# Decoder kernel on one core: row tiles in the second attention's weighting, weight preparation moved out of the stages' beginnings, semaphores cleared by the next stage, lead-in in another order

## The chip, the core and the metric

The kernel runs on one core of a Trainium2 chip. The metric is the device time of one execution in microseconds, the median of three runs. All weights and activations come in as fp32 in DRAM, and the output is fp32.

## The reference

Sixteen sequences of 112 tokens with 1024 features go through two decoder layers, each with a self part, a cross attention with 32 heads over 375 context rows, and a feed-forward part, each with a layernorm behind it:

```
x = _layernorm(x + _L0_attn_ref(x, mask, weight, bias))       # one linear, 32x32 blocks of the weight masked out
x = _layernorm(x + _L0_xattn_ref(x, ctx, ctx, 0, mask_ff0))   # 32 heads of 32, 8 key/value heads, 375 context rows
x = _layernorm(x + _L0_ffn_ref(x, Wq, Wr, aux_keys, aux_values, Wvd, Wvu, Wu1, ...))   # top 8 of 256 slots, gated
x = _layernorm(x + _L1_attn_ref(x, weight_qkv, weight_proj))  # 32 heads of 128, 8 key/value heads, causal over 16
x = _layernorm(x + _L1_xattn_ref(x, ctx, ctx, 0, mask_ff0))
x = _layernorm(x + _L1_ffn_ref(x, A_w, B_w, Wq_w, keys))      # 64 experts of rank 8, top 16
```

In `_L0_attn_ref` a 32x32 block of the weight counts if the sum of the int32 mask over it is above zero. In `_L1_attn_ref` the attention runs over the axis of 16 sequences, so that for each of the 112 positions there is a causal 16x16 table of probabilities per head, and

```
attn = softmax(where(causal, q k^T / sqrt(128), min))
out  = (attn v).reshape(S, B, 32*128) @ weight_proj.T
```

## The kernel before

Linears are computed in fp32 by three products of parts: each operand is split into a high part, rounded to the fp32r format, and a low part, the rest; high times high, high times low and low times high are summed in PSUM. Each such product is one pass of TensorE (a `MATMUL` row each). A few small products are plain fp32, which show two `MATMUL` rows each.

`build` runs three stages, one behind the other, each with its own semaphores and on-chip buffers: `token_stage` for layer 0 (from the start to about 847 us), `self_attention` for layer 1 (to about 2689 us), and `token_stage` for layer 1 (to the end). Behind each stage the helper `stage` runs a block in which GpSimd clears the stage's semaphores one by one (L1682 to L1686), and the next stage's engines start behind it.

**token_stage.** It starts with a preparation (L176 to L321) in a block of its own, which every engine leaves at L321 before the main part begins. SP loads chunks of 128 rows in the order of `part_of` into six stage buffers, which are the buffers `attn`, `row`, `xnew`, `xcur`, `probs` and `masked` of the main part (L238). In layer 0 the chunks are eight of the int32 mask, sixteen of Wu1 and Wq, and eight of the linear's weight. DVE sums the mask chunks (L311), ACT makes high parts (L250), DVE the low ones (L319), and for the linear's weight DVE multiplies by the block mask first (L314). In between PE and DVE compute the small tables of the slot router (L257 to L294), whose inputs ACT's queue loads (`small`). In layer 1 the chunks are the expert matrices A (eight) and B (four), and PE computes the router's keys (L269).

The main part is software-pipelined over turns t = -2 to B+1 = 17. Each of 16 sequences goes through its steps in several turns, and in a turn each engine runs 32 steps n, one per head of sequence t: scores (PE L545), mask and row minimum (DVE L835), exp (ACT L747), transposes of the probabilities (PE L550, copied at ACT L742 or DVE L829) and their product with V (PE L564). The other work of the neighbours, the first linear of sequence t+2 (PE L536), its layernorm (L510, L518), the queries (L527), keys, the feed-forward part (L646 to L674 on PE, L890 to L925 on DVE) stands between the heads at fixed n. SP's queue carries all loads and stores of a turn in a hand-written order: in turn t it loads x and its transpose for t+2, keys and queries from DRAM in layouts repeated for the heads (L370, L387), stores new queries and context parts (L380, L410), and loads `xcur` (L424), the row that is added to the heads' output. The scores of turn t start when queries (t, half 0) have landed; DVE has the row `L_masked L835 <- DMA L_xcur` where a turn's DVE work waits for `xcur`.

**self_attention.** The 1792 rows are taken as two halves of seven chunks of 128 rows; a chunk holds 8 positions of 16 sequences. A group G is one key/value head of a half, 16 in all. A group has units K, V and four Q, each a product of the half's rows with a 1024x128 weight (L1309, 24 passes of 512 columns and 24 of 384, `product` called from `unit`). Then `scores` (L1330) with 32-column tiles for the block-diagonal scores, `softmax` on DVE (L1564 to L1582, with ACT's exp L1451) and a stream transpose that gives `probsT`, whose entries outside the 32x32 blocks on the diagonal are zero. The next part runs in `project`, during the next group, right after its K unit:

```
1345  pe.matmul(bank("pv", G, c), val[:, c, :], probsT[:, :, c, :], start=True, stop=True).then_inc(pv_ok, 1)
```

one for each chunk c, into a ring of three PSUM banks that the projection uses too. ACT takes the high part (L1465), DVE the low (L1587, `low_weighted`), into three buffers `o_hi` and `o_lo`, and PE multiplies by the projection weights (L1358, 24 passes of 512 columns for each chunk), DVE adds to the rows (L1599). The PE order is weigh(0), weigh(1), project(0), weigh(2), project(1) and so on. GpSimd splits all weights of the stage from two raw buffers which SP loads (L1254, L1256, one split 3.4 us), in the order of the list `splits`.

Before group 0 stands a lead-in: gate and row data are loaded (L1189 to L1200), for each of seven chunks ACT doubles the row (`twice`, L1422), DVE adds the gated slot values that PE made from 64-row tiles (L1283, L1538) and takes the statistics, GpSimd the root, ACT normalizes (L1426), PE transposes (L1297), and ACT and DVE split (L1439, L1557).

## Time and profile before

| | us |
|---|---|
| median of 3 runs | 3425.71 |
| the runs | 3422.53, 3425.71, 3430.13 |
| the profiled execution, its own time | 3425.54 |
| its span | 3423.8 |
| PE busy | 3172.0 (93%) |
| weight loads busy | 2604.7 (76%) |
| DVE busy | 1849.2 (54%) |
| ACT busy | 1322.2 (39%) |
| POOL busy | 833.0 (24%) |

Columns of a timeline row are start, duration, engine, line, operation, output and input, shape and count, and in brackets the idle time before it with what ended it. Matmuls are pipelined, so the distance of two starts says what one costs, and the duration includes its tail. An engine with a q behind its name is its sequencer, which issues DMAs and waits on semaphores. GB/s is what the DMA engines moved, and DMA share how busy the 16 of them were. PEclk of 1.00 is 2.4 GHz and 0.50 is 1.2 GHz.

### The profile page before, as it was taken

The numbers are of one execution on the slowest core, as the hardware profiler recorded it, in microseconds if no ns is written. First come the engines' busy times: TensorE is split into PE (matmuls) and PEld (weight loads), VectorE is DVE, ScalarE is ACT, GpSimd is POOL, SyncE is SP. The second block draws the span as 40 slices with busy tenths as digits, with TensorE's granted clock in tenths as the row PEclk, the third lists the DMA queues.
The fourth block names the chain that finished last, engine by engine and source line by source line (L and its number), as shares of the span: only waits on it lengthen the run. The fifth ranks groups of instructions, "written<-read, shape, count | busy, mean of one in ns | idle before, by whom it ended". The sixth has DMA issues, their size and how long they took to land. (4 is left out here: it accounts for less than half of the span.)

```text
span 3423.8 us, 65971 instructions
## 1 busy us (share of the span) xinstructions
PE 3172.0 (93%) x25336; PEld 2604.7 (76%) x25336; DVE 1849.2 (54%) x4739; ACT 1322.2 (39%) x3550; POOL 833.0 (24%) x729
## 2 busy tenths in 40 slices
PE   3899999996799999999999999999999499999997
PEld 2777877775488887888878888888887378888886
DVE  4688888885443324333343323332333388888886
ACT  2577777774311111111111111111111287777774
POOL 0122222211234322432234322432232001000100
PEclk9999999997699999999999999999999799999999
DMA  5877777761322112221143111211111476655551
GB/s 181 218 177 184 172 178 181 179 171 40 94 86 87 52 53 68 87 74 44 56 154 130 45 36 50 62 52 42 38 56 31 141 175 153 152 149 144 145 138 45
DMA packets 209449, 370.01 MB, mean 108 GB/s; under 512 B 27009, under 2 KB 160737, under 8 KB 209138
## 3 DMA queue, kind: packets, MB, share of 16 engines
q1 hardware_dynamic: 205392, 363.01, 39.0%
q8 instruction: 203, 3.33, 0.4%
q10 hardware_dynamic: 3746, 2.79, 0.3%
q14 instruction: 108, 0.88, 0.1%
HBM read 283.20 MB, written 82.52 MB: 107 GB/s over the span
## 5 line engine op out<-in xcount | busy, mean ns | idle before, releaser
L747 ACT ACTIVATE L_probs<-L_masked,L_least 112x375 f32<-112x375 f32 x1024 | 624.8, 612 | 105.4 <-DVE L_least L835 102.1
L835 DVE CUSTOM_DVE_ANT_0 L_masked<-L_scores,L_nmask 112x375 f32<-112x375 f32 x1024 | 550.8, 543 | 158.2 <-PE L_scores L545 120.5
L1309 PE MATMUL sa_feat<-sa_x_hi,sa_w_hi 128*128 128x512 f32 (+1 forms) x1536 | 567.1, 369 | 1.8 <-DVE sa_x_lo L1557 1.8
L1309 PE MATMUL sa_feat<-sa_x_hi,sa_w_lo 128*128 128x512 f32 (+1 forms) x1536 | 561.4, 365 | 0.0
L1309 PE MATMUL sa_feat<-sa_x_lo,sa_w_hi 128*128 128x512 f32 (+1 forms) x1536 | 560.1, 365 | 0.0
L550 PEld LDWEIGHTS L_turned<-L_ident,L_probs 112*125 112x125 f32 x3072 | 456.3, 190 | 129.7 <-issue 46.5
L550 PE MATMUL L_turned<-L_ident,L_probs 112*125 112x112 f32 x3072 | 533.2, 283 | 19.5 <-DVE L_probsT L829 16.0
L545 PE MATMUL L_scores<-L_krep,L_qrep 128*112 128x376 f32 x1024 | 418.5, 410 | 6.8 <-DMA L_qrep<-query_parts 6.3
L1358 PE MATMUL sa_ring<-sa_p_hi,sa_o_hi 128*128 128x512 f32 x896 | 387.8, 433 | 8.3 <-issue 8.3
L742 ACT COPY L_probsT<-L_turned 125x336 f32<-125x336 f32 x672 | 293.2, 436 | 228.2 <-PE L_turned L550 227.5
L1599 DVE TENSOR_TENSOR sa_acc<-sa_acc,sa_ring 128x512 f32<-128x512 f32 x224 | 154.2, 688 | 414.8 <-PE sa_ring L1358 414.8
L1358 PE MATMUL sa_ring<-sa_p_lo,sa_o_hi 128*128 128x512 f32 x896 | 354.2, 395 | 0.0
L1358 PE MATMUL sa_ring<-sa_p_hi,sa_o_lo 128*128 128x512 f32 x896 | 354.1, 395 | 0.0
L1564 DVE SCALAR_TENSOR_TENSOR sa_sm<-sa_score,sa_causal 128x224 f32<-128x224 f32 x64 | 25.0, 391 | 549.8 <-PE sa_score L1330 549.8
L1309 PEld LDWEIGHTS sa_feat<-sa_x_hi,sa_w_hi 128*128 128x128 f32 x1536 | 289.7, 189 | 40.3 <-issue 6.8
L1309 PEld LDWEIGHTS sa_feat<-sa_x_hi,sa_w_lo 128*128 128x128 f32 x1536 | 289.3, 188 | 31.5
L1309 PEld LDWEIGHTS sa_feat<-sa_x_lo,sa_w_hi 128*128 128x128 f32 x1536 | 289.6, 189 | 30.3
L1465 ACT CAST sa_o_hi<-sa_ring 128x512 fp32r<-128x512 f32 x112 | 65.7, 586 | 496.8 <-PE sa_ring L1345 496.8
L467 POOL TENSOR_TENSOR L_attn<-L_attn,L_xcur 112x512 f32<-112x512 f32 x64 | 82.3, 1286 | 630.0 <-DVEq L848 630.0
L1256 POOL TENSOR_TENSOR sa_w_lo<-sa_raw,sa_w_hi 128x1024 fp32r<-128x1024 f32 x96 | 230.1, 2397 | 14.5 <-issue 1.0
L1358 PEld LDWEIGHTS sa_ring<-sa_p_hi,sa_o_hi 128*128 128x128 f32 x896 | 168.5, 188 | 78.0 <-issue 41.3
L1254 POOL CAST sa_p_hi<-sa_raw 128x1024 fp32r<-128x1024 f32 x64 | 68.6, 1073 | 604.9 <-PE sa_ring L1358 594.9
(305 smaller groups left out, 5240.9 us busy)
## 6 DMA issues: line engine op xcount, KB each, us to landing
L_qrep<-query_parts SPq DMA_DIRECT2D x256, 224.0 KB, 6.2
sa_raw<-in_wqkvU_dram SPq DMA_DIRECT2D x96, 512.0 KB, 3.6
L_krep<-ctx_parts SPq DMA_DIRECT2D x256, 188.0 KB, 4.3
sa_raw<-in_wprojU_dram SPq DMA_DIRECT2D x64, 512.0 KB, 3.6
query_parts<-L_qT_hi SPq DMA_DIRECT2D x64, 224.0 KB, 6.5
query_parts<-L_qT_lo SPq DMA_DIRECT2D x64, 224.0 KB, 6.8
L_xcur<-x SPq DMA_DIRECT2D x32, 448.0 KB, 5.0
L_val<-in_ctx_dram SPq DMA_DIRECT2D x64, 187.5 KB
```

The lines of the kernel that those rows point to most:

```text
L467: p.tensor_tensor(attn[0:S, cols], attn[0:S, cols], xcur[0:S, cols], ALU.add).then_inc(sum_ok, 1)
L545: pe.matmul(scores[0:S, (NH * t + n) % 3, 0:TP], qrep[:, gq, r, gi, :], krep[:, 4 * gq + gi, :], start=True, stop=True).then_inc(score_ok, 1)
L550: mm = pe.transpose(turned[0:TC, m % 2, S * j:S * j + S], probs[0:S, m % 4, TC * j:TC * j + TC], ident[0:S, 0:S])
L742: nc.scalar.copy(probsT[:, m % 8, :, :], turned[0:TC, m % 2, 0:TJ * S].rearrange("p (j s) -> p j s", s=S)).then_inc(copied_s, 1)
L747: nc.scalar.activation(probs[0:S, e % 4, :], masked[0:S, e % 4, :], ACT.Exp, bias=least[0:S, e:e + 1], scale=-1.0, accum_out=rsum[0:S, e:e ...
L835: v.tensor_tensor_reduce(out=masked[0:S, n % 4, :], in0=scores[0:S, (NH * t + n) % 3, 0:T], in1=nmask[0:S, :], scale=1.0, scalar=HUGE, op0 ...
L1254: nc.gpsimd.tensor_copy(hi, src)
L1256: nc.gpsimd.tensor_tensor(lo, src, hi.bitcast(F32), ALU.subtract).then_inc(p_ok if u is None else unit_ok, 1)
L1309: mm = pe.matmul(feat[:, u % 2, i, 0:t.stop - t.start], a[:, u % 2, k, :], b[:, k, t], start=(n == 0), stop=(n == 3 * KT - 1))
L1358: mm = pe.matmul(out, a[:, j, c % 3, :], b[:, j, 512 * h:512 * h + 512], start=(i == 0), stop=(i == 3 * QPG - 1))
L1465: nc.scalar.copy(o_hi[:, :, c % 3, :], ring[:, slot["pv", G, c][0], :].rearrange("p (j t) -> p j t", j=QPG)).then_inc(o_hi_ok, 1)
L1599: v.tensor_tensor(acc[:, c, cols], acc[:, c, cols], ring[:, b, :], ALU.add).then_inc(ring_free[b], 1)
```

## The change

**Row tiles.** `weigh` computes each chunk by four matmuls, one for each 32 rows of the chunk, which write 128 columns each to four PSUM banks. The zeros outside the diagonal blocks are left out. The PSUM tensors are one, `banks`; the four target banks are those of `feat` and `score`, so the ring holds the projection alone; `o_hi` and `o_lo` have two buffers. The first `weigh` of a group stands inside the second product of the next group's K unit, the others each one projection ahead, behind a wait for the low part of the chunk before. ACT signals `key_ok` after the first half of K.

```diff
@@ weigh
-                pe.matmul(bank("pv", G, c), val[:, c, :], probsT[:, :, c, :], start=True, stop=True).then_inc(pv_ok, 1)
+                    if not ends_half(G):
+                        pe.wait_ge(key_ok, G + 2)
+                else:
+                    pe.wait_ge(o_lo_ok, NC * G + c)
+                for p in range(4):
+                    q = slice(32 * p, 32 * p + 32)
+                    mm = pe.matmul(banks[:, 1 + p, 0:P], val[q, c, :], probsT[q, :, c, q], start=True, stop=True)
+                mm.then_inc(pv_ok, 1)
@@ project
-                weigh(G, 0)
-                weigh(G, 1)
+                if ends_half(G):
+                    weigh(G, 0)
                 pe.wait_ge(p_ok, QPG * (G + 1))
                 for c in range(NC):
-                    pe.wait_ge(o_lo_ok, NC * G + c + 1)
+                    if c + 1 < NC:
+                        weigh(G, c + 1)
+                    else:
+                        pe.wait_ge(o_lo_ok, NC * G + c + 1)
@@ K unit of the next group
-                        unit(G, K_UNIT, lambda: scores(G - 1, QPG - 1))
+                        unit(G, K_UNIT, lambda: scores(G - 1, QPG - 1), {6: lambda: weigh(G - 1, 0)})
```

On PE, at the end of the K unit of group 1 (`sa_feat` and `sa_banks` are the PSUM tensors of the attention before and after, `sa_probsT` the transposed probabilities), the order before is

```order
L1309 MATMUL sa_feat<-sa_x_hi,sa_w_lo 128x384
L1345 MATMUL sa_ring<-sa_probsT,sa_val 128x512 x2
L1358 MATMUL sa_ring<-sa_p_hi,sa_o_hi 128x512
L1358 MATMUL sa_ring<-sa_p_lo,sa_o_hi 128x512
L1358 MATMUL sa_ring<-sa_p_hi,sa_o_lo 128x512
```

and after it is

```order
L1409 MATMUL sa_banks<-sa_x_hi,sa_w_lo 128x384
L1451 MATMUL sa_banks<-sa_probsT,sa_val 128x128 x4
L1409 MATMUL sa_banks<-sa_x_hi,sa_w_hi 128x384
L1409 MATMUL sa_banks<-sa_x_lo,sa_w_hi 128x384
L1409 MATMUL sa_banks<-sa_x_hi,sa_w_lo 128x384
L1409 MATMUL sa_banks<-sa_x_hi,sa_w_hi 128x384
L1409 MATMUL sa_banks<-sa_x_lo,sa_w_hi 128x384
L1409 MATMUL sa_banks<-sa_x_hi,sa_w_lo 128x384
L1451 MATMUL sa_banks<-sa_probsT,sa_val 128x128 x4
L1468 MATMUL sa_banks<-sa_p_hi,sa_o_hi 128x512
```

The group's first weighting has moved ahead of the last six passes of K, and the second now waits for the low part of the first.

**Preparation, layer 0.** The block is gone. At turn -2 SP loads the transposed x, eight mask chunks and eight weight chunks; DVE runs `masked_weights`, ACT `high_weights`, and PE `first_linear`, which follows the chunks k by k for both halves of the output. The tables and Wu1, Wq are loaded in turn 0, split there by GpSimd, and PE and ACT compute the small tables at fixed heads of turn 0 (`slot_tables`).

```diff
+            def load_tables():
+                sp.wait_ge(chunk_done, 2 * KT)
+                for k in range(2):
+                    sp.dma_start(wu_raw[k], io["wu1T"][512 * k:512 * k + 512].rearrange("(k p) n -> p k n", p=P)).then_inc(ld_u, 16)
+                sp.dma_start(wq_raw, io["wqT"].rearrange("(k p) n -> p k n", p=P)).then_inc(ld_u, 16)
+                for dst, src in tables:
+                    sp.dma_start(dst, src).then_inc(ld_tables, 16)
...
+            def slot_tables(n):
+                if n == 14:
+                    pe.wait_ge(ld_tables, 16 * len(tables))
+                    pe.matmul(spare[0:48, 0:SLOTS], wrT[:], keysT[:], start=True, stop=True).then_inc(rk_ok, 1)
+                if n == 18:
+                    pe.wait_ge(rkT_ok, 1)
+                if n in (18, 20):
+                    j = n // 20
+                    for k in range(KT):
+                        mm = pe.matmul(spare[:, BOT * j:BOT * j + BOT], valT[k][:, P * j:P * j + P], wvdT[:, k, :],
+                                       start=(k == 0), stop=(k == KT - 1))
...
+            def first_linear(w):
+                pe.wait_ge(split_x, w.next(split_x))
+                for k in range(KT):
+                    pe.wait_ge(chunk_done, KT + k + 1)
+                    for h, bank in enumerate((spare, wide[:, 1, :])):
+                        mm = products(bank[0:S, :], (x_hi, x_lo), (w0_hi, w0_lo), slice(512 * h, 512 * h + 512), KT,
+                                      3 * k, 3 * k + 3)
```

On SP, in turn 0 of layer 0, the queries of sequence 1's second half are stored and `xcur` is loaded behind the second load of keys and queries. Before:

```order
L387 DMA L_qrep<-query_parts 32x4x448 x4
L380 DMA query_parts<-L_qT_hi 128x448
L380 DMA query_parts<-L_qT_lo 128x448
L380 DMA query_parts<-L_qT_hi 128x448
L380 DMA query_parts<-L_qT_lo 128x448
L410 DMA ctx_parts<-L_c_hi 128x376 x2
L410 DMA ctx_parts<-L_c_lo 128x376 x2
L412 DMA L_craw<-in_ctxT_dram 128x750
L374 DMA L_val<-in_ctx_dram 125x3x128
L424 DMA L_xcur<-x 112x1024
```

After:

```order
L271 DMA L_qrep<-query_parts 32x4x448 x4
L289 DMA L_attn<-in_wu1T_dram 128x4x256
L289 DMA L_row<-in_wu1T_dram 128x4x256
L290 DMA L_oT<-in_wqT_dram 128x8x64
L292 DMA L_wrT<-in_wrT_dram 64x48
L292 DMA L_keysT<-in_keysT_dram 64x256
...
L292 DMA L_ra<-in_valuesT_dram 128x256 x2
L264 DMA query_parts<-L_qT_hi 128x448
L264 DMA query_parts<-L_qT_lo 128x448
...
L332 DMA L_xcur<-x 112x1024
```

Nineteen loads, 2.95 MB, now stand ahead of those stores and of `xcur`.

**Preparation, layer 1.** GpSimd splits the expert matrices in groups 8 to 15 of the attention (eight more splits), SP stores both parts to DRAM (8 MB), and ACT's queue loads the parts of A at the start of turn 0 and those of B at the start of turn 1 of the last stage. The router's keys are computed at turn -1.

```diff
+        if G >= NKV:
+            splits.append((G, EXPERT, G - NKV))
...
+            def load_expert(i):
+                chunks = slice(4 * i, 4 * i + 4)
+                for dst, src in (((a_hi, "expert_hi"), (a_lo, "expert_lo")), ((b_hi, "expert_hi"), (b_lo, "expert_lo")))[i]:
+                    act.dma_start(dst[:].rearrange("p k n -> p (k n)").bitcast(F32),
+                                  io[src][:, chunks, :].rearrange("p m n -> p (m n)")).then_inc((ld_a, ld_b)[i], 16)
```

**Semaphores.** No block stands between the stages. GpSimd clears those of layer 0's stage in the attention's group 2, those of the attention at the start of the last stage, and those of the last stage at the end.

```diff
-            fn(*args, sem)
-            with nc.Block() as block:
-                @block.gpsimd
-                def _(pool):
-                    for one in used:
-                        pool.sem_clear(one)
...
+    held0, sems0 = stage(token_stage, nc, 0, io, [])
+    held1, sems1 = stage(self_attention, nc, io, sems0)
+    held0.close()
+    held2, sems2 = stage(token_stage, nc, 1, io, sems1)
```

**Lead-in of the attention.** `twice` and the later doubling at half 1 are gone (the gate is halved and the epsilon of these layernorms is a quarter, which gives the same normalized rows). The gate's data are loaded first, the first weights earlier, and GpSimd splits the first two units before it takes the roots.

## Rows read from the trace of the kernel before

**Rows 1.** The page: span, and busy time of the first engine.
```profile
span 3423.8 us, 65971 instructions
...
PE 3172.0 (93%) x25336; PEld 2604.7 (76%) x25336; DVE 1849.2 (54%) x4739; ACT 1322.2 (39%) x3550; POOL 833.0 (24%) x729
```

**Rows 2.** Timeline of DVE, from the start to the first layernorm.
```profile
14.84 1.22 DVE L311 TENSOR_REDUCE L_once_brow<-L_row 128x32 f32<-128x1024 int32 x1 [0.25 <-DMA L_row<-in_bmaskT_dram]
...
34.37 1.23 DVE L314 TENSOR_TENSOR L_attn<-L_attn,L_once_bm 128x1024 f32<-128x1024 f32 x1
...
51.60 1.23 DVE L319 TENSOR_TENSOR L_w_lo<-L_row,L_w_hi 128x1024 fp32r<-128x1024 f32 x1
...
76.08 2.55 DVE L518 TENSOR_SCALAR L_xnew<-L_xb,L_mv,L_rstd 112x1024 f32<-112x1024 f32 x1 [1.06 <-POOL L_rstd L462]
```

**Rows 3.** Timeline of PE, the same stretch.
```profile
22.96 1.22 PE L257 MATMUL L_wide<-L_once_brow,L_once_blocks 128*128 128x256 f32 x2 [22.96 <-DMA L_nmask<-in_mask_dram]
...
59.86 0.77 PE L536 MATMUL L_spare<-L_w_hi,L_x_hi 128*112 128x512 f32 x1 [26.02 <-POOL L_x_lo L503]
```

**Rows 4.** Table by stretches: window, length, busy times, PEclk, DMA share, GB/s.
```profile
0.00:26.00 26.00, 3.04 (x8) 1.61 (x9) 13.21 (x23) 4.56 (x13) 0.19 (x4) 1.00 0.91 301
...
100.00:130.00 30.00, 29.41 (x232) 24.13 (x233) 16.52 (x51) 18.87 (x55) 2.52 (x2) 0.86 0.97 235
130.00:145.00 15.00, 10.62 (x102) 8.40 (x100) 13.62 (x36) 10.90 (x33) 4.10 (x4) 0.92 0.40 99
```

**Rows 5.** Waits of DVE in 100 to 145 us: total, times, longest.
```profile
DVE L_masked L835 <- DMA L_xcur<-x: 3.4, 1, 3.4
```

**Rows 6.** Waits of SP's queue, the whole span.
```profile
SPq L1682 <- PEq L1682: 17.1, 3, 6.4
```

**Rows 7.** Timeline of PE in the attention's lead-in.
```profile
861.92 0.59 PE L1366 MATMUL sa_feat<-sa_lsum,sa_ones 128*128 128x1 f32 x2 [15.78 <-ACT sa_lv L1475]
...
865.38 3.78 PE L1283 MATMUL sa_ring<-sa_wvu,sa_zT 64*128 64x512 f32 x6
...
876.55 3.78 PE L1283 MATMUL sa_ring<-sa_wvu,sa_zT 64*128 64x512 f32 x4
```

**Rows 8.** Timeline of PE in group 3, scores and weighting.
```profile
1306.17 1.09 PE L1297 MATMUL sa_ring<-sa_ident,sa_late 128*128 128x128 f32 x8
1307.02 0.48 PE L1309 MATMUL sa_feat<-sa_x_hi,sa_w_hi 128*128 128x512 f32 x1
...
1316.58 0.40 PE L1309 MATMUL sa_feat<-sa_x_hi,sa_w_lo 128*128 128x512 f32 x1
1316.91 0.70 PE L1330 MATMUL sa_score<-sa_kT,sa_qT 128*32 128x32 f32 x56
1317.54 0.50 PE L1309 MATMUL sa_feat<-sa_x_hi,sa_w_hi 128*128 128x512 f32 x1
...
1333.40 1.02 PE L1345 MATMUL sa_ring<-sa_probsT,sa_val 128*128 128x512 f32 x2
...
1334.49 0.40 PE L1358 MATMUL sa_ring<-sa_p_lo,sa_o_hi 128*128 128x512 f32 x1
...
1339.86 1.02 PE L1345 MATMUL sa_ring<-sa_probsT,sa_val 128*128 128x512 f32 x2
```

**Rows 9.** Timeline of DVE in group 2: a softmax step beside GpSimd's work.
```profile
1186.04 2.28 DVE L1570 TENSOR_TENSOR sa_sm<-sa_sm,sa_most 128x224 f32<-128x224 f32 x1
```

**Rows 10.** Timeline of PE and SP at the last stage's beginning.
```profile
2721.49 1.01 PE L527 MATMUL L_wide<-L_ident,L_xnew 112*128 112x112 f32 x4 [14.02 <-DMA L_xnew<-x]
...
2697.02 0.33 SPq L238 DMA_DIRECT2D L_attn<-in_awT_dram  x1
...
2717.63 0.34 SPq L416 DMA_DIRECT2D L_xnew<-x  x1
```

**Rows 11.** Table by stretches, turn 0 and turn 1 of the last stage.
```profile
2725.00:2765.00 40.00, 24.86 (x240) 20.37 (x240) 20.46 (x70) 23.71 (x75) 1.28 (x1) 0.73 0.93 216
2765.00:2795.00 30.00, 27.92 (x329) 23.03 (x328) 23.95 (x78) 25.62 (x80) 2.06 (x3) 1.00 0.79 186
```

More of the change, by code:

```diff
@@ L222, in token_stage @@
-        small += [(ident[:], io["ident"]), (nmask[0:S, :], io["mask"])]
-        small_in, chunk_done, prep_pe, prep_dve = s("small_in"), s("chunk_done"), s("prep_pe"), s("prep_dve")
-        chunk_in = [s(f"chunk_in{i}") for i in range(NST)]
-        chunk_masked, chunk_hi = s("chunk_masked"), s("chunk_hi")
-        prep = once.enter_context(nc.Block())
-        def chunk(i):
-            what = part_of[i][2]
-            raw = stage[i % NST][:, 0:part_of[i][1]]
-            return raw.bitcast(I32) if what == "sum" else raw
@@ L401, in body @@
                     load_queries(t, 1)
+                if first and t == 0:
+                    load_tables()
                 if on(1):
@@ L504, in body @@
                     pool.drain().then_inc(xt_free, 1)
+            for one in stale:
+                pool.sem_clear(one)
             turns(pool, body)
@@ L803, in routed_ffn, with load_small, high_weights @@
                     nc.scalar.copy(z_hi[:, :, :], spare[:, 0:4 * S].rearrange("p (j s) -> p j s", s=S)).then_inc(z_hi_ok, 1)
+            def load_small():
+                if first:
+                    act.dma_start(blocks[:], io["blocks"]).then_inc(ld_blocks, 16)
+                for dst, src in small:
+                    act.dma_start(dst, src).then_inc(small_in, 16)
+            def high_weights():
+                for k in range(KT):
+                    act.wait_ge(chunk_masked, k + 1)
+                    nc.scalar.copy(w0_hi[:, k, :], stage[(KT + k) % NST]).then_inc(chunk_hi, 1)
@@ L813, in body @@
                         routed_ffn(w, n, on)
+            load_small()
             turns(act, body)
@@ L1026, in body @@
                         routed_ffn(t, w, n, on)
+            v.memset(half[:], -0.5)
             if first:
+                for part in (c_hi, c_lo):
+                    v.memset(part[:, :, T:TP].bitcast(F32), 0.0)
+                v.memset(qaug[BOT:BOT + 1, :], 1.0)
                 dve.sem_inc(z_stored, 16)
@@ L1218, in _ @@
                 load_raw(i)
+                store_experts(i - 2)
+            for i in range(len(splits) - 2, len(splits)):
+                store_experts(i)
             store_rows(1)
+            sp.wait_ge(expert_stored, 32 * 8)
             sp.wait_ge(stored, 2 * 16 * NC)
@@ L1321, in unit @@
                 product(G, u, 0, {3: landed})
-                product(G, u, 1)
+                product(G, u, 1, later)
             def scores(G, j):
@@ L1475, in _, with take_z @@
             nc.scalar.activation(lv[:], pair[:, :, 1], ACT.Ln, bias=1.0, scale=1.0, accum_out=lsum[:]).then_inc(log_ok, 1)
-            for half in range(2):
+            def take_z(half):
                 act.wait_ge(z_ok, half + 1)
```

425 lines of the change are left out of this document (240 added, 185 removed).

## The prediction, made before the changed kernel ran

> **What bounds the kernel.** The page comes first. TensorE is busy for 3172.0 of 3423.8 us [rows 1], so the time is TensorE's own work plus about 250 us in which it waits, and a change pays where it takes passes off TensorE or shortens one of those waits. The timelines then say where the waits are: at the beginnings of the three stages. At the start the matmuls of the first linear begin at 59.86, behind 26.02 us of idle [rows 3]; between 2697 and 2721 the last stage has almost nothing but its preparation [rows 10]; the clearing blocks take 17.1 us of SP's time in three waits [rows 6]. Last I read what one chunk of the attention's weighting costs [rows 8]. The profiled execution took 3425.54 us and the median is 3425.71, so the sum made against the first holds for the second.
>
> **Layer 0's preparation.** Before, the mask sums of DVE end at 14.84 + 1.22 = 16.1, but the product with the block matrix starts at 22.96, since PE waited for all small loads [rows 2, 3], and the first masked weight chunk is made at 34.37, behind the splits of Wu1 and Wq and the small tables. Now nothing stands between: 16.1, plus 1.2 for the product, 0.4 for the comparison and some signals, and 1 us for the transposed x that is loaded first, makes about 19. The 16 DVE steps from 34.37 to 52.8 take 18.5 us [rows 2] and stay, ending at 37 to 38. The loads keep pace: some 8.9 MB (sixteen chunks of 512 KB, x and the small ones) at 301 GB/s [rows 4] are 30 us, and the last chunk is wanted at about 34. PE follows chunk by chunk with six passes each, so behind the last chunk stand six passes (0.77 us at most, [rows 3]) instead of 48, and two instead of one statistics. Before, from the last low part to the layernorm L518 there were 76.08 - 52.8 = 23.3 us; I take 5.5 (the six passes with their tail some 3, the second statistics and the root, for which L518 waited 1.06 us [rows 2], the rest). The layernorm then starts at about 43 in place of 76.08: **-33 us** (-36 to -28). What follows it, up to the first scores, is a chain through DRAM and is the same.
>
> **The tables in turn 0.** Nineteen loads with 2.95 MB are issued ahead of the query stores and of `xcur`. Just there the DMA engines are 0.97 busy at 235 GB/s [rows 4], so the loads delay the others by 2.95 / 0.235 = 12.6 us, if nothing gives. Behind them, 130 to 145 us has a share of 0.40, and that slack could take some; against it, PE now waits at head 14 for every table, with 18 heads of the turn behind it, and DVE already waited 3.4 us for `xcur` there [rows 5], which comes later now. GpSimd's six split steps on 128x1024 and 128x512 are hidden unless the turn is held by them. **+13** (+6 to +20). If the loads fitted in the slack this would be nothing, if they came as slowly as small rows can it would be 20.
>
> **Boundary 0 to 1.** The clears leave the path between the stages: one of the three waits, the longest, is 6.4 us [rows 6]. **-6.4.** In group 2 GpSimd clears them in the time that it waits for TensorE anyway.
>
> **Attention's lead-in.** Seven ACT doublings go, and loads and splits come sooner, but the chain per chunk goes through DVE, GpSimd's root, ACT, PE and back. The roots now wait for two splits of 3.4 us. **-3** (-7 to +3).
>
> **The row tiles.** From 1334.49 to the next weighting at 1339.86 stand 23 passes, 0.2335 us each; the period of a chunk is 1339.86 - 1333.40 = 6.46, and less 24 passes (5.60) the weighting costs 0.86 us [rows 8]. That is two fp32 passes of 512 columns. Now it is four matmuls of 128 columns, eight passes. A pass of 128 columns costs 0.85 / 8 = 0.106 (eight L1297 between 1306.17 and 1307.02). If the four tiles ran together it would be 2 x 0.106 = 0.21; if one after the other, 0.85. Do tiles of different rows run together here? Six L1283 in the lead-in, on both row halves, take 3.78 us, and four on one half also 3.78 [rows 7], so yes, at least two. A change of tiling has a price: the scores with 32-column tiles start 0.33 after the pass before, where 0.23 is usual, and the next pass is 0.63 behind, of which some 0.1 again is the way back [rows 8]; with two changes that is 0.2. So 0.21 + 0.2 = 0.41 at the least, and with 0.1 for what eight issues and loads in four groups add I take 0.50, near the lower end since both rows show tiles running together. The saving is 0.36 x 112 = **-40 us** (-50 with 0.41; with 0.63 as in the first rival -26).
>
> The Trainium skill, TensorE: Matmul & The Clock Gate, Part 3 (packing small matmuls), gives 3.07x for four row tiles of 512 columns, not 4x; the estimate from that page would be 0.85 / 3.07 + 0.2 = 0.48 and the same saving within 2 us. TensorEngine Tiling, Key Properties, says that changing the tiling mode drains TensorE; the trace agrees by the 0.1 us at each side of the scores, and a drain that cost more would be the last rival.
>
> The wait behind a group's first weighting, for its high and low part, stays about as long: before, the second weighting's 0.86 us stood in it, now six passes of K with 384 columns do, 6 x 0.2335 x 384 / 512 = 1.05 us. In the other chunks the low part is made during the projection before. But the first weighting also stands 1.05 us sooner behind the softmax, which is longer where GpSimd works beside it: one of its steps takes 2.28 us then [rows 9], and groups 8 to 15 get a GpSimd split more. If each of 14 groups lost all of the 1.05 it would be 15; with the splits in one group of two and hitting the last softmax seldom I take **+2** (0 to +7).
>
> **Boundary 1 to 2.** Before, SP's first load of the stage is at 2697.02 and that of `xnew`, which starts the real work, at 2717.63 [rows 10]. The preparation's 19.2 us between (less 1.4 for issues that stay) go, and the clears: the two other waits share 17.1 - 6.4 = 10.7 us [rows 6], 5.3 each. **-24.5** (-27 to -19).
>
> **Expert parts in turns 0 and 1.** Each of these turns gets 4 MB more. In turn 0 DMA is 0.93 busy at 216 GB/s, in turn 1 0.79 [rows 11]. Loads of 128 wide rows move faster than that mixture, at 301 GB/s [rows 4]: 4 MB are 13.3 us. In turn 0 I count all of them but two, since queries and keys come later by that much; in turn 1 the idle share of 0.21 over some 40 us takes 8.4 of them, and I count 3 of the rest. **+14** (+5 to +24). Final clears of fewer semaphores: **-0.4**.
>
> **Sum.** -33 + 13 - 6.4 - 3 - 40 + 2 - 24.5 + 14 - 0.4 = -78.3, that is 3425.5 - 78.3 = **3347 us**.
>
> **Rivals.**
> First, the tiles' weight loads go one after the other (eight of about half of 0.106 us) and only the streaming overlaps: 0.43 + 0.2 = 0.63 us per chunk, saving 26, not 40: 3361. For it: no row shows two weight loads at once, and the L1283 rows with long streams would look alike in both cases; against it nothing but the forecast's simplicity, so it gets a good chance.
> Second, no overlap at all: 0.85 + 0.2 = 1.05, +21 in place of -40: 3347 + 61 = 3408. The L1283 rows speak against it, but they are two tiles of 64 rows at 1.2 GHz, not four of 32.
> Third, the other side: every row tile waits until the one before has drained. A lone small pass takes 0.59 / 2 = 0.295 us [rows 7]; eight are 2.4 us for a chunk, +1.5 each, 168 us in all: 3347 + 40 + 168 = 3555. It decides for slower as soon as a chunk's weighting costs more than 0.86 + 38.3 / 112 = 1.20 us.
> Fourth, the moved loads cost nothing (the turns have slack after all): 3347 - 27 = 3320. Or they cost double, since turn 0 holds up everything behind it: 3374. The shares of 0.40 to 0.97 [rows 4, 11] leave both open.
> That the gain at the beginnings isn't there (the first scores wait for something else, as for keys) is part of the second half of that.
>
> **Chances.** Forecast with its neighbours 0.50, weight loads in series 0.20, no overlap 0.07, draining 0.04, moved loads nearly free 0.09, loads double 0.10. Terms added at their good ends give about 3312, at their bad ends with the first rival about 3390; the range is 3308 to 3390, which leaves out draining, most of no overlap, and the far ends of the loads. Some 0.2% is 7 us, about what a measurement can tell from no change; only 0.02 of the chance falls there, between the second and third rivals. Faster 0.93, same 0.02, slower 0.05.
>
> **What would show it.** The successor of the layernorm L518 at 43 us and all that follows it 33 us sooner; turn 0 of the first stage some 13 us longer; the attention's first K product 9 us sooner against the end of the stage before; a chunk period of 6.1 us in the projection, and about 0.5 from a row of four tiles to the next pass; the last stage's first transpose, at 2721.49 before [rows 10], some 24 us sooner against the attention's end. A chunk period above 6.3, or beginnings that come sooner while the turns behind them grow by as much, would make the prediction wrong.

## The result, and the profile after

| | before | changed |
|---|---|---|
| median, us | 3426.45 (4 runs) | 3375.59 (4 runs) |
| all runs, us | 3422.53, 3425.71, 3427.20, 3430.13 | 3370.88, 3371.77, 3379.40, 3379.68 |
| profiled execution, its span | 3425.54, 3423.8 | 3379.68, 3377.9 |
| ratio changed to before | | 0.9847, 95% interval 0.9834 to 0.9859 |

The changed kernel is 51 us faster. The forecast was 78 us faster, 3347, with a range of 3308 to 3390: sign and range hold, and 27 us of the expected gain are missing. The question of this section is where they went. The page of the changed kernel, as [rows 1]:

```profile
span 3377.9 us, 67066 instructions
...
PE 3153.8 (93%) x26008; PEld 2601.9 (77%) x26008; DVE 1861.0 (55%) x4698; ACT 1304.2 (39%) x3520; POOL 872.9 (26%) x751
```

TensorE has 18 us less to do (3172.0 before), so more than half of the gain is less waiting. A ladder of marks, the same places read in both timelines, gives each part's share. "First scores" is the start of DVE's first step on them, and the attention's products are the high times high passes of K, V and Q. The column "changed again" is a second profiled execution of the changed kernel (`changed_again`, 3368.71 us, below).

| stretch | before | changed | changed again | predicted change |
|---|---|---|---|---|
| start to the first scores | 101.7 | 70.1 | 70.2 | -33 |
| turn 0 of layer 0 | 42.9 | 60.4 | 58.8 | +13 |
| turns 1 to 14 | 629.3 | 629.5 | 630.9 | 0 |
| turn 15's first scores to the attention's first product | 134.8 | 125.5 | 125.5 | -9.4 |
| to its last K, V or Q product | 1721.0 | 1693.4 | 1689.5 | -38 |
| to the last stage's first scores | 110.9 | 87.7 | 86.3 | -24.5 |
| its turns 0 and 1 | 65.4 | 88.4 | 88.6 | +14 |
| turns 2 to 14 | 533.8 | 533.4 | 533.5 | 0 |
| turn 15's first scores to the end of DVE | 74.3 | 80.2 | 74.2 | 0 |

**The beginning.** Timeline of DVE of the changed kernel, as [rows 2]:

```profile
15.75 1.22 DVE L1048 TENSOR_REDUCE L_brow<-L_row 128x32 f32<-128x1024 int32 x1
...
18.85 1.23 DVE L1063 TENSOR_TENSOR L_xnew<-L_xnew,L_bm 128x1024 f32<-128x1024 f32 x1
...
36.01 2.25 DVE L1056 TENSOR_TENSOR L_w_lo<-L_xcur,L_w_hi 128x1024 fp32r<-128x1024 f32 x1
...
43.73 2.55 DVE L444 TENSOR_SCALAR L_xnew<-L_xb,L_mv,L_rstd 112x1024 f32<-112x1024 f32 x1 [1.06 <-POOL L_rstd L370]
```

The first masked chunk is made at 18.85 (19 predicted), the last low part ends at 38.3 (37 to 38), the layernorm starts at 43.73 (43). The only surprise is the last low part, 2.25 us instead of 1.22. GpSimd adds the bias beside it, but the two DVE steps before it lie beside the same work and took 1.21 us each, so the cause isn't shown.

**Turn 0 of layer 0.** Waits of PE between 69 and 131 us, with total, times and longest:

```profile
PE L_spare L543 <- DMA L_ra<-in_valuesT_dram: 11.4, 1, 11.4
PE L_wide L453 <- DVE L_xnew L444: 5.6, 1, 5.6
```

L543 is the first of the small tables at head 14, and it stands 11.4 us for the last of the nineteen loads. Table by stretches, columns as [rows 4]:

```profile
35.00:45.00 10.00, 3.74 (x14) 1.94 (x13) 8.68 (x9) 1.91 (x2) 6.51 (x5) 0.96 0.00 0
75.00:95.00 20.00, 12.67 (x114) 10.38 (x112) 9.66 (x28) 8.91 (x27) 5.39 (x4) 0.93 1.02 210
```

The DMA share is 1.02 while the tables are waited for, and 0.00 in a stretch some 30 us before they are asked for.

**The weighting.** Timeline of PE in the attention, changed kernel, as [rows 8]:

```profile
1302.75 0.40 PE L1468 MATMUL sa_banks<-sa_p_hi,sa_o_lo 128*128 128x512 f32 x1
1303.08 0.50 PE L1451 MATMUL sa_banks<-sa_probsT,sa_val 32*128 32x128 f32 x8
1303.51 0.50 PE L1468 MATMUL sa_banks<-sa_p_hi,sa_o_hi 128*128 128x512 f32 x1
1303.85 0.39 PE L1468 MATMUL sa_banks<-sa_p_lo,sa_o_hi 128*128 128x512 f32 x1
...
1309.30 0.50 PE L1451 MATMUL sa_banks<-sa_probsT,sa_val 32*128 32x128 f32 x8
```

A chunk's period is 1309.30 - 1303.08 = 6.22 us (6.46 before), and less 24 x 0.2335 the weighting costs 0.62 us, where 0.50 was predicted. The eight passes take 0.43 to the next full pass. The rest stands on the two sides: 0.33 from the pass before, where 0.23 is usual, and again 0.34 behind the first full pass.

**Turns 0 and 1 of the last stage.** DMA issues of the changed kernel between 2656 and 2667 us, with count, KB of each and the time to landing:

```profile
L_a_hi<-expert_hi ACTq DMA_DIRECT2D x1, 2048.0 KB, 15.0
L_a_lo<-expert_lo ACTq DMA_DIRECT2D x1, 2048.0 KB, 22.6
L_qrep<-query_parts SPq DMA_DIRECT2D x4, 224.0 KB, 8.4
L_krep<-ctx_parts SPq DMA_DIRECT2D x4, 188.0 KB, 20.6
```

and of the kernel before at the same place of its turn, 2727 to 2737 us:

```profile
L_krep<-ctx_parts SPq DMA_DIRECT2D x8, 188.0 KB, 7.4
L_qrep<-query_parts SPq DMA_DIRECT2D x5, 224.0 KB, 7.8
```

The keys of the second half, issued in the same microseconds as the two large loads, take 20.6 us instead of 7.4. (Before, the median is over eight key loads, with the changed kernel over four.) PE waits for the queries queued behind them (total, times and longest, 2628 to 2760 us):

```profile
PE L_scores L471 <- DMA L_qrep<-query_parts: 13.6, 2, 6.9
```

**The end.** The profiled execution is one of the two long ones. Table by stretches of the changed kernel, from some 42 us behind the last turn's first scores:

```profile
3330.00:3338.00 8.00, 7.49 (x60) 5.27 (x57) 3.95 (x8) 1.17 (x3) 1.29 (x1) 1.00 0.00 0
3338.00:3346.00 8.00, 5.70 (x27) 4.38 (x26) 5.00 (x9) 1.06 (x2) 1.56 (x4) 0.72 0.19 58
3346.00:3354.00 8.00, 8.00 (x33) 6.56 (x33) 2.41 (x13) 0.35 (x1) 0.00 (x0) 0.64 0.01 3
```

The granted clock falls from 2.4 to 1.2 GHz within the second stretch; PE was busy for 7.49 of 8 us in the first and for 5.70 in the second. The profile of the kernel before has 2.4 GHz at the same place, and its last stretch is 5.9 us shorter (74.3 us against 80.2).

### The profile page after: what moved, and what is told of

It reads as the page before. It is cut to its first block and busy times, and to the rows that moved or that the text cites. A ratio compares the mean times of both kernels' runs of the same rounds, so it can differ in the third digit from the quotient of the medians.

```text
span 3377.9 us, 67066 instructions
## 1 busy us (share of the span) xinstructions
PE 3153.8 (93%) x26008; PEld 2601.9 (77%) x26008; DVE 1861.0 (55%) x4698; ACT 1304.2 (39%) x3520; POOL 872.9 (26%) x751
## 5 line engine op out<-in xcount | busy, mean ns | idle before, releaser
L1409 PE MATMUL sa_banks<-sa_x_hi,sa_w_hi 128*128 128x512 f32 (+1 forms) x1536 | 568.6, 370 | 1.8 <-DVE sa_x_lo L1661 1.8
L1409 PE MATMUL sa_banks<-sa_x_hi,sa_w_lo 128*128 128x512 f32 (+1 forms) x1536 | 561.4, 366 | 0.0
L1409 PE MATMUL sa_banks<-sa_x_lo,sa_w_hi 128*128 128x512 f32 (+1 forms) x1536 | 560.0, 365 | 0.0
L471 PE MATMUL L_scores<-L_krep,L_qrep 128*112 128x376 f32 x1024 | 419.8, 411 | 17.1 <-DMA L_qrep<-query_parts 13.6
L1468 PE MATMUL sa_banks<-sa_p_hi,sa_o_hi 128*128 128x512 f32 x896 | 366.0, 408 | 0.0
L1468 PE MATMUL sa_banks<-sa_p_lo,sa_o_hi 128*128 128x512 f32 x896 | 356.1, 397 | 0.0
L1468 PE MATMUL sa_banks<-sa_p_hi,sa_o_lo 128*128 128x512 f32 x896 | 355.8, 397 | 0.0
L1409 PEld LDWEIGHTS sa_banks<-sa_x_hi,sa_w_hi 128*128 128x128 f32 x1536 | 289.6, 189 | 42.0 <-issue 6.8
L1409 PEld LDWEIGHTS sa_banks<-sa_x_hi,sa_w_lo 128*128 128x128 f32 x1536 | 289.3, 188 | 31.6
L1409 PEld LDWEIGHTS sa_banks<-sa_x_lo,sa_w_hi 128*128 128x128 f32 x1536 | 289.5, 188 | 30.2
L490 PE MATMUL L_wide<-L_probsT,L_val 125*32 125x112 f32 x6144 | 203.3, 266 | 8.5 <-DMA L_val<-in_ctx_dram 7.9
```

What stands on the lines that cost most here:

```text
L471: pe.matmul(scores[0:S, (NH * t + n) % 3, 0:TP], qrep[:, gq, r, gi, :], krep[:, 4 * gq + gi, :], start=True, stop=True).then_inc(score_ok, 1)
L490: mm = pe.matmul(wide[HD * gi:HD * gi + HD, gq, S * r:S * r + S], val[:, j, HD * g:HD * g + HD], probsT[:, (4 * u + gi) % 8, j, :], start= ...
L1409: mm = pe.matmul(feat[u % 2][i][:, 0:t.stop - t.start], a[:, u % 2, k, :], b[:, k, t], start=(n == 0), stop=(n == 3 * KT - 1))
L1468: mm = pe.matmul(out, a[:, j, c % 2, :], b[:, j, 512 * h:512 * h + 512], start=(i == 0), stop=(i == 3 * QPG - 1))
```

## The experiments

**Row tiles undone, places kept** (`full_rows`):

```diff
-                    mm = pe.matmul(banks[:, 1 + p, 0:P], val[q, c, :], probsT[q, :, c, q], start=True, stop=True)
+                    mm = pe.matmul(banks[:, 1 + p, 0:P], val[:, c, :], probsT[:, :, c, q], start=True, stop=True)
```

> The changed kernel with one edit: each of the four weighting matmuls of a chunk takes all 128 rows (the same 128 output columns, the zeros outside the diagonal blocks included), so no row tiles; places, banks and waits stay. In the changed kernel's profile a chunk of the projection has a period of 6.22 us, of which the weighting is 0.62. Theory A (row tiles gain only in that a load and a stream of different rows overlap, and the eight weight loads come one after the other): eight whole passes of 0.106 us each without change of tiling are 0.85 us, the chunk's period 6.45, 112 x 0.23 = 26 us more than the changed kernel. Theory B (the gain in the attention comes from the new places and the projection's own ring, not from the tiles): the period stays near 6.22 and the time within 5 us of the changed kernel.

Measured: 3415.12 us, ratio to before 0.9958 (0.9944 to 0.9972), against 3371.46 for the changed kernel on the same chip, 44 us slower. Its chunk:

```profile
1308.00 1.05 PE L1451 MATMUL sa_banks<-sa_probsT,sa_val 128*128 128x128 f32 x8
1308.81 0.48 PE L1468 MATMUL sa_banks<-sa_p_hi,sa_o_hi 128*128 128x512 f32 x1
...
1314.49 1.05 PE L1451 MATMUL sa_banks<-sa_probsT,sa_val 128*128 128x128 f32 x8
```

The period is 6.49, more than the 6.45 expected; no wait shows in it. From first to last product the attention takes 1728.7 us: 39.2 more than in `changed_again` and 35.3 more than in the first profile of the changed kernel, and 7.7 more than the kernel before. A part of each difference is the clock: this profile has 1.2 GHz for 21.7 us of the attention, `changed_again` for 13.6, the first profile for 18.9 and the kernel before for 15.6. If such a stretch costs half of its length (an estimate; `changed_again` shows it below), the tiles alone are worth about 34 to 35 us, and the new places and banks cost about 5 without them. What they cost is 0.035 us of each chunk's period and a wait of 0.45 us for the low part before each group's second weighting. Another 5 us of the whole difference are the clock at the end (79.0 us behind the last turn's first scores, not 74.2). Theory B is out. Theory A has the period nearly right and the time not (26 us), and its reason is wrong, as the next runs show.

**One row tile for all four** (`one_group`):

```diff
+                    mm = pe.matmul(banks[:, 1 + p, 0:P], val[0:32, c, :], probsT[0:32, :, c, q], start=True, stop=True)
```

> The changed kernel, but all four weighting matmuls of a chunk take rows 0 to 31 of the values and of the probabilities, so that all lie on one row tile (three quarters of the weighted values are thus not the reference's). If different row tiles are what makes them overlap: eight passes of about 0.106 us, 0.85 plus 0.2 for two changes of tiling, a chunk's period of 6.65 us, and 48 us more in all. If a tile of 32 rows is cheaper in itself, wherever it lies: the period stays 6.22.

Measured in one execution: 3445.68 us, 74 us above the changed kernel, period 6.88:

```profile
1315.11 1.15 PE L1451 MATMUL sa_banks<-sa_probsT,sa_val 32*128 32x128 f32 x8
1316.19 0.50 PE L1468 MATMUL sa_banks<-sa_p_hi,sa_o_hi 128*128 128x512 f32 x1
...
1321.99 1.15 PE L1451 MATMUL sa_banks<-sa_probsT,sa_val 32*128 32x128 f32 x8
```

A tile of 32 rows isn't cheaper in itself; different rows are the gain. It costs even 0.23 us more than expected. The single records say where: the first two passes start 0.213 us apart, the other six 0.110 to 0.112. One weight load, 0.107 us, isn't hidden behind the change of tiling; the next run shows that it is the first pass's own. On the way back another isn't hidden, that of the full matrix.

**Streams twice as wide** (`wide_stream`):

```diff
+                    w = slice(64 * (p // 2), 64 * (p // 2) + 64)
+                    mm = pe.matmul(banks[:, 1 + p, 0:2 * P], val[q, c, :], probsT[q, :, c, w], start=True, stop=True)
```

> The changed kernel, but each row tile's matmul streams 256 columns instead of 128 (twice as many tokens of the chunk; the copies take the first 128, so the weighted values are not the reference's). The weight loads are as before. Theory A (the eight weight loads of 128 columns in series set the 0.43 us between the first tile and the next full pass; streams of different tiles overlap): the chunk's period grows by under 0.1 us, mostly the tail of the last tile. Theory C (the streams themselves come one after the other and loads are hidden behind them): 8 x 0.053 = 0.43 us more per chunk, period 6.65, 48 us in all.

Measured in one execution: 3397.14 us, 26 above the changed kernel; period 6.44, 0.22 more:

```profile
1304.28 0.71 PE L1452 MATMUL sa_banks<-sa_probsT,sa_val 32*128 32x256 f32 x8
1304.92 0.50 PE L1469 MATMUL sa_banks<-sa_p_hi,sa_o_hi 128*128 128x512 f32 x1
...
1310.71 0.71 PE L1452 MATMUL sa_banks<-sa_probsT,sa_val 32*128 32x256 f32 x8
```

Neither theory: A wanted under 0.1, C 0.43. It is 0.107 for each of two passes, so two streams are on the path, not eight and not none. The records of `changed_again` fit that. One row from each of four timelines, of the weight loads and of PE, with windows that hold the first pass alone, then the second alone:

```profile
1306.72 0.20 PEld L1451 LDWEIGHTS sa_banks<-sa_probsT,sa_val 32*128 32x128 f32 x4 [0.36 <-issue]
1306.73 0.39 PE L1451 MATMUL sa_banks<-sa_probsT,sa_val 32*128 32x128 f32 x4
1306.83 0.20 PEld L1451 LDWEIGHTS sa_banks<-sa_probsT,sa_val 32*128 32x128 f32 x4
1306.94 0.29 PE L1451 MATMUL sa_banks<-sa_probsT,sa_val 32*128 32x128 f32 x4
```

Within 0.02 us all four tiles have their loads and their matmuls under way, each 7 ns behind the one before. The second loads start at 1306.833 to .853, the second matmuls at 1306.940 to .960. So the four tiles run wholly side by side, loads too. These two passes alone allow two readings of the first 0.213 us: stream, then the second load, or the first load, then the stream with the second load beside it. The wide run decides, by the same rows:

```profile
1304.28 0.20 PEld L1452 LDWEIGHTS sa_banks<-sa_probsT,sa_val 32*128 32x128 f32 x4 [0.37 <-issue]
1304.38 0.20 PEld L1452 LDWEIGHTS sa_banks<-sa_probsT,sa_val 32*128 32x128 f32 x4
1304.60 0.39 PE L1452 MATMUL sa_banks<-sa_probsT,sa_val 32*128 32x256 f32 x4
```

The second loads start 0.11 us behind the first here too, though the streams are twice as long, and the second matmuls 0.21 us behind these loads, the length of a stream of 256 columns. So the second loads run beside the first streams, and what isn't hidden is the first load, with which the first matmul's record begins. What the path sees in the changed kernel is about 0.09 us until the pass before is through, load 0.107, two streams of 0.107, about 0.09 again, and the load of the next full matrix, 0.11, which wasn't made ahead either: together the 0.62. The expectation of the next run takes the first reading.

**The tiles twice** (`two_sets`): this tells whether the load shows in every pass or only behind a change of tiling.

```diff
-                for p in range(4):
+                for p in (0, 1, 2, 3, 0, 1, 2, 3):
```

> The changed kernel, but each chunk's four row tiles are computed twice, one set right behind the other (the second overwrites the first with the same values). The chunk's period is 6.22 us now; in its trace the four tiles of a pass start 7 ns apart, their loads too, the second pass starts 0.213 us behind the first, and 0.107 of this is the second pass's weight load, which starts only when the first pass has streamed. Theory L (each pass of a row tile shows its weight load): 2 x 0.213 = 0.43 us more per chunk, period 6.65. Theory F (the load shows only once, in the first pair behind a change of tiling, since nothing could be loaded ahead; after that 0.107 to 0.112 a pass, as on the single row tile): 0.21 to 0.24 more, period 6.45.

Measured in one execution: 3403.00 us; periods of 6.455 us (rows of the same timeline):

```profile
1305.63 0.73 PE L1451 MATMUL sa_banks<-sa_probsT,sa_val 32*128 32x128 f32 x16
...
1312.09 0.73 PE L1451 MATMUL sa_banks<-sa_probsT,sa_val 32*128 32x128 f32 x16
```

Theory F, to the hundredth: +0.235. A second set of four tiles costs 0.11 per pass, since its loads run under the streams of the first. Of the 0.62 us of a chunk's weighting, two streams are 0.21; the rest is what two changes of tiling cost, among it two loads of 0.11 that aren't hidden.

**The changed kernel again** (`changed_again`):

> The changed kernel itself, beside the others on the same chip, as their measure. Its four executions so far fall in two pairs, 3371 and 3379.5 us; the profiled one was of the longer kind and shows a granted clock of 1.2 GHz between 3341 and 3352 us, where the kernel before still had 2.4 GHz. If the pairs come from that alone, these executions again lie at one or the other, and a profile of the shorter kind shows no such fall and about 74 us from the last turn's first scores to the end, not 80.

Measured: 3368.71, 3370.00, 3372.92 and 3380.27 us, median 3371.46, ratio 0.9838 (0.9823 to 0.9853). The profiled execution took 3368.71:

```profile
3325.00:3333.00 8.00, 7.49 (x60) 5.27 (x57) 3.98 (x8) 1.13 (x3) 1.29 (x1) 1.00 0.00 0
3333.00:3341.00 8.00, 5.70 (x42) 4.57 (x41) 5.01 (x10) 1.07 (x2) 1.56 (x4) 1.00 0.19 58
3341.00:3349.00 8.00, 5.94 (x27) 4.13 (x27) 3.69 (x15) 0.88 (x2) 0.00 (x0) 1.00 0.01 2
```

The same stretch, the same busy time of 7.49 and 5.70 us, and the clock stays at 2.4 GHz; 74.2 us to the end. So the same program with the same load is granted either clock there, and this makes times some 6 us apart.

The attention was 3.9 us shorter in this profile too (1689.5 against 1693.4), and that is the granted clock as well. Table by stretches, 885.4 to 890.4 and 904 to 908 us, first of the changed kernel, then of `changed_again`, whose attention begins at the same time within 0.03 us:

```profile
885.40:890.40 5.00, 5.00 (x13) 3.86 (x13) 3.06 (x7) 1.45 (x2) 2.08 (x6) 0.50 0.00 0
904.00:908.00 4.00, 4.00 (x16) 4.00 (x15) 0.00 (x0) 0.00 (x0) 0.00 (x0) 0.57 0.00 0
```

```profile
885.40:890.40 5.00, 5.00 (x16) 3.98 (x16) 3.03 (x7) 1.47 (x2) 2.10 (x6) 0.66 0.00 0
904.00:908.00 4.00, 4.00 (x25) 4.00 (x24) 0.00 (x0) 0.48 (x1) 0.71 (x1) 1.00 0.00 0
```

The rise to 2.4 GHz comes 1.9 us sooner and gives 0.9 us, the fall for 3.4 us at 904 doesn't come and gives 1.6, and between the halves the first projection has six passes fewer at 1.2 GHz (0.43 us each instead of 0.23), 1.2 us: 3.7 of the 3.9. The profiles of the other runs with this weighting fall into the same two kinds: 1692.8 to 1693.4 us with that fall (`tables_early`, `both_moved`, `both_again`), 1689.6 to 1690.5 without it (`expert_moved`, `own_clears`, `all_early`). What decides between the two grants stays open.

**Tables at turn -2** (`tables_early`): the loop over `tables` moves out of `load_tables` into a function that SP calls behind the context load of turn -2.

```diff
+                if first and t == -2:
+                    load_small_tables()
```

> The changed kernel, but the sixteen small tables (1.6 MB: the values' parts, wvdT, the router's) are loaded by SP at turn -2, behind the linear's weight chunks and the first context rows, and only Wu1 and Wq (1.3 MB) stay in turn 0. In the changed kernel turn 0 lasts 58.8 to 60.4 us against 42.9 before, PE waits 11.4 us in it for the tables, and the DMA share is 0.00 between 35 and 45 us. Theory A (turn 0 is long because the tables are late for head 14, and because the bytes keep queries and xcur back): the first scores stay within 1 us of 70, turn 0 falls to 45 to 50, and the time by 9 to 14 us. Theory B (turn 0 is bound by the other loads, 1.0 of DMA share, and PE's wait would only be followed by another): turn 0 falls by less than 5 us.

Measured: 3360.18 us, ratio 0.9811 (0.9796 to 0.9826). Turn 0 is 49.1 us, the first scores at 70.3: Theory A, about 11 us by the medians and 10 to 11 by turn 0. PE's wait for tables is gone, and the next one shows (waits of DVE, 69 to 131 us, as [rows 5]):

```profile
DVE L_masked L868 <- DMA L_xcur<-x: 7.3, 1, 7.3
```

**Expert parts at the stage's start and in turn 1's middle** (`expert_moved`):

```diff
             def load_small():
...
+                if not first:
+                    load_expert(0)
...
-                if not first and t in (0, 1):
-                    load_expert(t)
                 for n in range(NH):
+                    if not first and t == 1 and n == 16:
+                        load_expert(1)
```

> The changed kernel, but ACT's queue loads the parts of A (4 MB) right behind the small loads at the last stage's start, where the DMA share is 0.14 to 0.66, and those of B at head 16 of turn 1, where the queues are empty, instead of at the starts of turns 0 and 1. In the changed kernel these turns last 43 and 45.6 us against 27.7 and 37.7 before; a key load that took 5 us takes up to 22 beside A's. Theory A (the bursts stand in the way of keys and queries just when these are awaited): turn 0 falls to 28 to 32 and turn 1 to 38 to 40, the first scores come 0 to 8 us later, and the time falls by 13 to 20 us. Theory B (the bytes cost their time wherever they are, since everything up to turn 2 is bound by DMA): what turn 0 gains the start loses, and the time falls by under 7 us.

Measured: 3355.90 us, ratio 0.9798 (0.9783 to 0.9812), 16 to 20 us below the changed kernel's two medians. Turns 0 and 1 last 30.5 and 37.7 us (before the change 27.7 and 37.7); the first scores come 5.6 us later. Theory A. In turn 0 the DMA issues of 2658 to 2668 us show keys at their old pace, 8.8 us where it was 20.6:

```profile
L_qrep<-query_parts SPq DMA_DIRECT2D x7, 224.0 KB, 8.3
L_krep<-ctx_parts SPq DMA_DIRECT2D x4, 188.0 KB, 8.8
```

The 8 MB still move, and cost 5.6 us before the first scores and 2.8 in turn 0, in place of the changed kernel's 23.

**Both** (`both_moved`):

> Both edits, tables at turn -2 and the expert parts at the stage's start and at head 16. They lie in different stages, so the gains add: by Theory A of both 22 to 34 us below the changed kernel, about 3343; by Theory B of both under 12.

Measured: 3349.07 us, ratio 0.9776 (0.9762 to 0.9791); about 22 to 26 below the changed kernel, at the low end of what was expected and 6 us above the 3343. By the marks the gains add: turn 0 of layer 0 lasts 48.1 us, and turns 0 and 1 of the last stage 31.1 and 37.7, as in the two runs with one edit each. A second series (`both_again`):

> The kernel with both edits once more, as the measure of the one beside it: 3346 to 3351 us.

Measured: 3348.55, ratio 0.9770 (0.9754 to 0.9787).

**The clears back between the stages** (`own_clears`): a block in which GpSimd clears the stage's semaphores, behind each of the first two stages, and nothing is cleared inside a stage.

```diff
+    clear(sems0)
...
-    held1, sems1 = stage(self_attention, nc, io, sems0)
+    held1, sems1 = stage(self_attention, nc, io, [])
+    clear(sems1)
```

> The changed kernel with the two clearing blocks of before between the stages again, GpSimd clearing nothing inside a stage. The prediction put the two at 6.4 and 5.3 us: 11.7 us slower than the changed kernel. If the clears stood beside a wait that is there anyway (the last stores, or the first loads of the next stage), under 4 us.

Measured: 3389.14 us, ratio 0.9892 (0.9875 to 0.9910). Waits of SP's queue, as [rows 6]; L1789 is the end of the two blocks between the stages, L1802 that of the last:

```profile
SPq L1789 <- PEq L1789: 11.8, 2, 7.4
SPq L1802 <- PEq L1802: 5.7, 1, 5.7
```

From turn 15 to the attention's first product it is 7.4 us longer than in `changed_again`, and from the last product to the last stage's first scores 4.4: together 11.8, as predicted. The two profiled executions differ by 19.5 us (3388.20 and 3368.71): besides the 11.8, this one had the low clock at the end, 80.6 us instead of 74.2, which is 6.4, and 1.3 lie in turn 0 of the last stage.

**Wu1 and Wq early too** (`all_early`): both edits, and

```diff
+                    load_small_tables()
+                    load_tables()
...
-                if first and t == 0:
-                    load_tables()
```

> Tables and expert parts moved as in the run with both edits (3349.1 us), and Wu1 and Wq too are loaded at turn -2, behind the tables, so that turn 0 has none of the moved loads. In that run turn 0 lasts 48.1 us against 42.9 before, DVE waits 6.6 us in it for xcur, and the DMA share is 0.00 between 40 and 45 us. If the rest of the loads keeps xcur back: turn 0 falls to 43 to 44.5 and the time by 4 to 6 us, to 3344. If turn 0 is now held by something else (the first linear's successor, GpSimd's splits): within 2 us of 3349.

Measured: 3341.46 us, ratio 0.9750 (0.9735 to 0.9766), 7 us below the run beside it and 87 below the kernel before on that chip: the best version here. DVE no longer waits for `xcur`, so the loads did keep it back. But turn 0 falls to 45.4 us (47.0 and 48.1 in the two profiles with both edits), not to the 43 to 44.5 that were expected, and 2.5 us above the kernel before stay unexplained. Of the difference to `both_again`, turn 0 is 1.6 us, the attention 3.2, the way into the last stage 2.0, and the end 1.5. Only the first has to do with the edit as far as the profiles show: the attention's is the fall of the clock told at `changed_again`, which `both_again` has (PEclk 0.61 from 891.5 to 895.5 us) and this profile hasn't (1.00).

## Why the prediction was right or wrong

**Layer 0's preparation**, -33: measured -31.6. Each mark of the chain came out within 1 us. That the splits and tables stood ahead of the masked weights only by order was read rightly.

**Tables in turn 0**, +13 (+6 to +20): measured +17.5 and +15.9. The term was bytes over the rate of the stretch, 12.6 us, and named PE's wait at head 14 as a thing against it without a price. The bytes were priced fairly: with only the 1.3 MB of Wu1 and Wq left in turn 0 (`tables_early`), it is 6.2 us longer than before, where 1.3 / 0.235 gives 5.5. Moving the other 1.6 MB gave 10 to 11 us back, where bytes over rate give 6.8. So this step was mis-sized by the 3 to 5 us that the wait adds: an engine that works in order stands at a fixed head, for 11.4 us, until the last of the tables has landed.

**Boundary and lead-in of the attention**, -9.4: measured -9.3. The clears are 7.4 of it by `own_clears`, so the lead-in's new order gave about 2 of the 3 predicted.

**Row tiles**, -40 + 2: measured -27.6 and -31.5, between which stands the clock. A chunk takes 0.24 us less, which for the 105 of 112 chunks that lie in this stretch are 25 us. The mis-sized step is "with 0.1 for what eight issues and loads in four groups add I take 0.50". It is 0.62. The number is that of the first rival (0.63, eight weight loads in series), but its mechanism is false: loads of different row tiles run side by side, 7 ns apart. The step took 0.1 on each side for the changes of tiling and 0.1 for everything else; two weight loads of 0.11 us, one on each side, are what nothing covers, and the four issues add only 0.02. That 0.62 is so near to the rival's 0.63 is chance. The Trainium skill, TensorE: Matmul & The Clock Gate, Part 3, says that a weight load overlaps with matmuls in flight only when the row group differs. For tiles of different rows the trace agrees as far as it goes: their loads run side by side, 7 ns apart. On a single tile (`one_group`) it doesn't: from the second pass on each load starts within 3 ns of the stream before it, on the same rows, and the passes are 0.11 us apart with nothing of a load between them. The Trainium skill, TensorEngine Tiling, Key Properties, says that a change of the tiling mode drains TensorE, and gives no price; the trace agrees, with about 0.1 us on each side and two loads of 0.11 us that aren't hidden. The drain as third rival (each tile waiting for the last) is refuted, and so is no overlap, though `one_group` shows what it would have cost: 1.28 us for a chunk, not 1.05, and 74 us against the changed kernel. The prediction asked for a chunk period of 6.1 us and called one above 6.3 a sign of being wrong; it is 6.22. Of the +2 for GpSimd's splits nothing shows: groups of the second half (106.3 us) gained as much against before (108.3) as those of the first (108.9 against 111.0).

**Boundary 1 to 2**, -24.5: measured -23.2 and -24.6; clears 4.4 of it where 5.3 was taken, the preparation 19 to 20.

**Expert parts**, +14 (+5 to +24): measured +23.0. The mis-sized step is "in turn 1 the idle share takes 8.4 of them". The idle time of turn 1 lies in its last third; the load is issued at its first head, where SP issues keys and queries too. `expert_moved` shows the same bytes costing 8 us. A share of idle time over a turn is cover only for a load that is issued into the idle part.

**The end**, 0: +5.9 or 0, by the granted clock. It was no term, and the same program shows both. The medians carry a part of it.

**The range.** Its ends were added up wrongly: the terms' good ends give 3310 and the bad ones with the first rival 3400, where the prediction says 3312 and 3390. The measured 3375.59 lies inside either way. That it does is in part luck: three terms missed by 3 to 12 us, and all in the same direction.

Against the profiled execution: 31.6 - 17.5 - 0.2 + 9.3 + 27.6 + 23.2 - 23.0 + 0.4 - 5.9 = 45.5 us, where the spans differ by 45.9. Of the 33 us to the predicted 78, 10 lie in the attention (6 to 7 by `changed_again`, whose clock fell less), 9 in the expert parts, 6 in the clock at the end, 5 in turn 0 of layer 0, and 3 in the rest.

## What to carry to other kernels

A load that is moved off one path has to be put where its queue is empty and well before an engine that works in order reaches its wait; look at the DMA share in stretches of 5 us, since the mean of a turn hides that its first half is full. Four row tiles of a small matmul run truly side by side, loads and streams, but a set between full passes costs, besides its streams, two weight loads that nothing hides, its own first one and that of the next full matrix, and about 0.1 us on each side, so collect tiles behind one change: a second set of four cost 0.235 us where the first cost 0.62. When a prediction's number agrees with a rival's, look at single records before taking over its mechanism. Before a difference of a few us between two profiles is put down to an edit, compare the granted clock of the same stretches: here it alone made 4 us in the attention and 6 at the end.

## What the runs showed of the hardware that wasn't expected

- The loads of four row tiles start 7 ns apart, and so do their matmuls; a set of four with two passes of 128 columns takes 0.62 us between full passes, a second set behind it 0.235, four on one tile 1.28, and eight full passes 0.89.
- A fp32 pass of 128 columns behind a change of tiling is followed by its neighbour on the same tile after 0.213 us, the ones after that after 0.11. With 256 columns the second load still starts 0.11 us behind the first, and the second matmul 0.32 behind the first: the load that isn't hidden is the first.
- Four loads of 188 KB took 20.6 us to land beside two 2 MB loads from another queue; such loads took 7.4 in the kernel before and 8.8 with the large ones moved away. The large ones took 15.0 and 22.6.
- The same stretch with the same busy TensorE (5.70 of 8 us) was granted 0.72 of the clock in one execution and 1.00 in another, and the end took 80.2 and 74.2 us.
- Some 19 us behind the attention's first product, with TensorE busy throughout and DVE idle, one execution was granted 0.57 over 4 us (16 passes) and another 1.00 (25 passes).
